# The first pair of a fused attention and feed-forward kernel: f32 and one batch at a time, with zero matmuls in TensorE's gaps

## The chip, the cores and the metric

The kernel runs on one core of a Trainium2 chip. The metric is the time of one execution on the device in microseconds (us), the median over several runs. Engines in the profile: PE is TensorE (matmuls), PEld its weight loads, DVE is VectorE, ACT is ScalarE, POOL is GpSimd, SP issues the DMAs.

## The reference, cut to what matters

There are 16 batches of 64 positions with 512 features. An autocorrelation attention comes first, with a gated residual, then a gated feed-forward part with a second one.

```python
x = x + jnp.tanh(g_xattn[0]) * autocorrelation(layernorm(x), ctx, ctx)   # Q, K, V; 8 heads, C = 2
x = x + jnp.tanh(g_ffn[0]) * ffn(layernorm(x), W_gate, W_up, W_down)

# autocorrelation, for every feature on its own, over L = 64 positions
corr = ifft(fft(q) * conj(fft(k))).real
w, idx = top_k(corr, 8);  w = softmax(w)
out = sum over i of w[i] * v[min(idx[i] + pos, L - 1)]
# ffn: 512 -> 1792 -> 512, weights in f16
h = silu(x @ W_gate.T) * (x @ W_up.T);  out = h @ W_down.T
```

## The kernel before, in words

Two batches of 64 rows fill the 128 partitions: this is a pair, and there are eight pairs, 0 to 7. All data of f32 accuracy goes to TensorE as two f16 halves, high and low. ScalarE makes the high half by a copy, GpSimd (or VectorE, where ON_VECTOR says so) makes the low half by subtracting. A product with a constant matrix, itself split in two, is then three f16 matmuls: high by high, low by high, high by low. The steps of one pair, by the names in the code:

- stats1, rstd1, q_norm: layernorm of x. q_hi, q_lo, k_hi, k_lo: the split of the normed x and of ctx.
- kspec, vspec, qspec (`transform`, L757): spectra of k, v and q, each six matmuls of 64 rows by 512 columns. The two batches of a pair lie in rows 0 to 63 and 64 to 127, so their matmuls use different halves of the array. kcopy, vcopy: ScalarE copies the spectra out of PSUM.
- prod, p_hi, p_lo, lags (L836 to L838): product of the spectra, split, and 24 matmuls of 64 columns that give the correlation.
- max, match, exp, sum, scale: the eight best lags of every row by VectorE (MAX8, MATCH_REPLACE8), their softmax on ScalarE, VectorE and GpSimd.
- wt, w_hi, w_lo for pair 0: transpose of the weights on TensorE. For the others w_rows_hi, w_rows_lo, w_t: split first, then two transposing DMAs.
- wspec, mix_prod, m_hi, m_lo, mix (L897): spectra of the weights, product with those of v, split, and 12 matmuls back to positions. residual: x1 = x + gate * result, with the second layernorm's sums.
- rstd2, xn, then xt, x_hi, x_lo (pair 0, by TensorE) or x_rows_hi, x_rows_lo, x_t (the others, by DMA): the normed x1, transposed and split.
- gate, up (`widen`, L773): 14 tiles of 128 hidden features in four steps by SPANS, each tile of each of the two weight matrices eight matmuls with 128 moving columns (the 128 tokens of the pair). tanh, silu, hid, h_hi, h_lo: the activation and its split. down (L937): 28 matmuls of 512 columns. out, store.

ORDER is one long list written into the file, in which the steps of several pairs are interleaved. Every engine walks the same list, takes the steps that are its own and does them strictly in that order, with semaphores between engines. So a step that waits holds back all later steps on its engine. PSUM has eight banks, assigned by hand (`k_bank` and the like), and a step also waits until its bank is free. SP first issues all loads (x and ctx of pair 0, f32 constants, x and ctx of pair 1, the f16 constants `consts`, then the weights `wg`, `wu`, `wd`), and then, in ORDER's place, the transposing DMAs and stores. The f32 constants `consts32` are loaded in the version before too, though nothing uses them there.

Of the kernel before, what the change touches and what calls it, by code (L numbers as in the profile page):

```python
# [114 lines left out]
mix_prod:0 exp:1 kspec:2 mix_prod:0.1 wspec:0.1 m_hi:0 sum:1 kcopy:2 m_hi:0.1 mix_prod:0.2 scale:1 mix:0
mix_prod:0.3 m_hi:0.2 m_lo:0 m_lo:0.1 m_hi:0.3 w_rows_hi:1 mix:0.1 scales:0 m_lo:0.3 m_lo:0.2 kcopy:2.1 w_t:1
vspec:2 stats1:3 w_rows_lo:1 mix:0.2 vcopy:2 residual:0 vcopy:2.1 rstd1:3 k_hi:3 qspec:2 w_t:1.1 prod:2
rstd2:0 prod:2.1 p_hi:2 xn:0 p_hi:2.1 p_lo:2 q_norm:3 xt:0 p_lo:2.1 x_hi:0 stats1:4 wspec:1 q_hi:3 x_lo:0
rstd1:4 lags:2 mix_prod:1 gate:0 q_lo:3 max:2 m_hi:1 m_lo:1 mix_prod:1.1 up:0 match:2 m_hi:1.1 k_lo:3 tanh:0
k_hi:4 gate:0.1 k_lo:4 silu:0 exp:2 m_lo:1.1 wspec:1.1 sum:2 kspec:3 mix_prod:1.2 scale:2 up:0.1 kcopy:3 hid:0  # L120
kcopy:3.1 mix_prod:1.3 tanh:0.1 vspec:3 m_hi:1.2 silu:0.1 w_rows_hi:2 m_lo:1.2 q_norm:4 gate:0.2 m_hi:1.3
w_t:2 hid:0.1 vcopy:3 m_lo:1.3 vcopy:3.1 mix:1 h_hi:0 mix:1.1 w_rows_lo:2 mix:1.2 tanh:0.2 qspec:3 residual:1
k_hi:5 h_lo:0 w_t:2.1 up:0.2 h_hi:0.1 prod:3 rstd2:1 silu:0.2 p_hi:3 gate:0.3 h_lo:0.1 prod:3.1 up:0.3
tanh:0.3 hid:0.2 p_lo:3 p_hi:3.1 xn:1 wspec:2 p_lo:3.1 down:0 silu:0.3 x_rows_hi:1 hid:0.3 h_hi:0.2 x_t:1
mix_prod:2 h_lo:0.2 m_hi:2 lags:3 h_hi:0.3 down:0.1 q_hi:4 x_rows_lo:1 max:3 h_lo:0.3 mix_prod:2.1 x_t:1.1
down:0.2 match:3 m_lo:2 m_hi:2.1 q_lo:4 down:0.3 wspec:2.1 m_lo:2.1 exp:3 kspec:4 mix_prod:2.2 gate:1 sum:3
m_hi:2.2 kcopy:4 m_lo:2.2 mix_prod:2.3 kcopy:4.1 up:1 tanh:1 scale:3 m_hi:2.3 silu:1 m_lo:2.3 stats1:5
w_rows_hi:3 vspec:4 w_t:3 hid:1 mix:2 k_lo:5 vcopy:4 mix:2.1 out:0 vcopy:4.1 mix:2.2 store:0 w_rows_lo:3
h_hi:1 qspec:4 gate:1.1 prod:4 rstd1:5 w_t:3.1 residual:2 up:1.1 tanh:1.1 rstd2:2 p_hi:4 silu:1.1 prod:4.1
p_lo:4 gate:1.2 hid:1.1 p_hi:4.1 xn:2 h_hi:1.1 p_lo:4.1 wspec:3 tanh:1.2 h_lo:1 x_rows_hi:2 up:1.2 mix_prod:3  # L130
x_t:2 mix_prod:3.1 m_hi:3 h_lo:1.1 silu:1.2 m_hi:3.1 lags:4 m_lo:3 hid:1.2 gate:1.3 max:4 h_hi:1.2 up:1.3
tanh:1.3 h_lo:1.2 stats1:6 down:1 x_rows_lo:2 silu:1.3 match:4 m_lo:3.1 down:1.1 x_t:2.1 hid:1.3 wspec:3.1
h_hi:1.3 kspec:5 exp:4 h_lo:1.3 mix_prod:3.2 down:1.2 mix_prod:3.3 m_hi:3.2 q_norm:5 m_hi:3.3 m_lo:3.2 sum:4
gate:2 q_hi:5 kcopy:5 scale:4 down:1.3 tanh:2 m_lo:3.3 kcopy:5.1 up:2 silu:2 w_rows_hi:4 out:1 w_t:4
w_rows_lo:4 vspec:5 hid:2 rstd1:6 mix:3 h_hi:2 mix:3.1 q_lo:5 k_hi:6 mix:3.2 vcopy:5 gate:2.1 residual:3
w_t:4.1 vcopy:5.1 stats1:7 up:2.1 rstd2:3 tanh:2.1 q_norm:6 h_lo:2 xn:3 qspec:5 rstd1:7 wspec:4 prod:5
gate:2.2 silu:2.1 p_hi:5 prod:5.1 k_hi:7 p_lo:5 hid:2.1 p_hi:5.1 up:2.2 q_norm:7 tanh:2.2 p_lo:5.1 x_rows_hi:3
mix_prod:4 h_hi:2.1 x_t:3 k_lo:6 gate:2.3 silu:2.2 store:1 q_hi:6 hid:2.2 lags:5 x_rows_lo:3 h_hi:2.2 up:2.3
max:5 tanh:2.3 h_lo:2.1 m_hi:4 down:2 silu:2.3 x_t:3.1 mix_prod:4.1 h_lo:2.2 hid:2.3 m_hi:4.1 down:2.1 match:5
q_lo:6 m_lo:4 down:2.2 m_lo:4.1 exp:5 kspec:6 q_hi:7 sum:5 wspec:4.1 h_hi:2.3 kcopy:6 h_lo:2.3 gate:3  # L140
mix_prod:4.2 scale:5 m_hi:4.2 k_lo:7 w_rows_hi:5 down:2.3 kcopy:6.1 up:3 m_lo:4.2 out:2 tanh:3 mix_prod:4.3
store:2 w_rows_lo:5 w_t:5 silu:3 m_hi:4.3 gate:3.1 hid:3 m_lo:4.3 vspec:6 tanh:3.1 mix:4 vcopy:6 w_t:5.1
mix:4.1 vcopy:6.1 mix:4.2 h_hi:3 up:3.1 residual:4 h_lo:3 silu:3.1 gate:3.2 rstd2:4 hid:3.1 xn:4 qspec:6
x_rows_hi:4 wspec:5 prod:6 h_hi:3.1 x_t:4 x_rows_lo:4 up:3.2 tanh:3.2 prod:6.1 p_hi:6 silu:3.2 p_lo:6
mix_prod:5 gate:3.3 hid:3.2 m_hi:5 h_lo:3.1 up:3.3 mix_prod:5.1 x_t:4.1 p_hi:6.1 h_hi:3.2 down:3 p_lo:6.1
tanh:3.3 m_hi:5.1 silu:3.3 hid:3.3 h_lo:3.2 wspec:5.1 lags:6 m_lo:5 mix_prod:5.2 down:3.1 mix_prod:5.3
m_hi:5.2 max:6 h_hi:3.3 m_hi:5.3 h_lo:3.3 down:3.2 match:6 m_lo:5.1 q_lo:7 gate:4 m_lo:5.2 exp:6 down:3.3
sum:6 kspec:7 out:3 scale:6 up:4 kcopy:7 m_lo:5.3 tanh:4 kcopy:7.1 silu:4 gate:4.1 w_rows_hi:6 hid:4 w_t:6
w_rows_lo:6 vspec:7 tanh:4.1 mix:5 vcopy:7 mix:5.1 vcopy:7.1 mix:5.2 h_hi:4 w_t:6.1 up:4.1 residual:5 h_lo:4
silu:4.1 rstd2:5 qspec:7 hid:4.1 gate:4.2 prod:7 h_hi:4.1 xn:5 p_hi:7 wspec:6 p_lo:7 prod:7.1 x_rows_hi:5  # L150
up:4.2 tanh:4.2 x_t:5 mix_prod:6 x_rows_lo:5 p_hi:7.1 mix_prod:6.1 silu:4.2 p_lo:7.1 gate:4.3 hid:4.2
wspec:6.1 h_lo:4.1 h_hi:4.2 x_t:5.1 m_hi:6 up:4.3 store:3 tanh:4.3 m_lo:6 lags:7 silu:4.3 down:4 max:7
h_lo:4.2 mix_prod:6.2 down:4.1 hid:4.3 match:7 h_hi:4.3 m_hi:6.1 gate:5 m_hi:6.2 m_lo:6.1 h_lo:4.3
mix_prod:6.3 down:4.2 tanh:5 m_lo:6.2 m_hi:6.3 exp:7 m_lo:6.3 up:5 sum:7 scale:7 down:4.3 mix:6 out:4
w_rows_hi:7 mix:6.1 mix:6.2 w_t:7 gate:5.1 residual:6 silu:5 up:5.1 rstd2:6 hid:5 w_rows_lo:7 xn:6 h_hi:5
gate:5.2 tanh:5.1 h_lo:5 w_t:7.1 silu:5.1 store:4 hid:5.1 up:5.2 tanh:5.2 x_rows_hi:6 silu:5.2 h_hi:5.1 x_t:6
x_rows_lo:6 gate:5.3 hid:5.2 h_lo:5.1 wspec:7 down:5 mix_prod:7 mix_prod:7.1 m_hi:7 x_t:6.1 tanh:5.3 m_lo:7
up:5.3 m_hi:7.1 silu:5.3 h_hi:5.2 wspec:7.1 m_lo:7.1 down:5.1 mix_prod:7.2 h_lo:5.2 hid:5.3 m_hi:7.2
mix_prod:7.3 m_lo:7.2 gate:6 m_hi:7.3 h_hi:5.3 m_lo:7.3 down:5.2 tanh:6 h_lo:5.3 silu:6 mix:7 mix:7.1 mix:7.2
down:5.3 up:6 out:5 residual:7 gate:6.1 hid:6 rstd2:7 up:6.1 xn:7 tanh:6.1 silu:6.1 x_rows_hi:7 h_hi:6 x_t:7  # L160
gate:6.2 x_rows_lo:7 hid:6.1 h_hi:6.1 h_lo:6 up:6.2 tanh:6.2 h_lo:6.1 silu:6.2 x_t:7.1 gate:6.3 store:5
hid:6.2 up:6.3 h_hi:6.2 tanh:6.3 h_lo:6.2 down:6 silu:6.3 hid:6.3 h_hi:6.3 h_lo:6.3 down:6.1 gate:7 down:6.2
tanh:7 down:6.3 up:7 out:6 silu:7 store:6 gate:7.1 hid:7 h_hi:7 h_lo:7 up:7.1 tanh:7.1 silu:7.1 gate:7.2
hid:7.1 up:7.2 tanh:7.2 h_hi:7.1 silu:7.2 h_lo:7.1 gate:7.3 hid:7.2 up:7.3 h_hi:7.2 tanh:7.3 h_lo:7.2 down:7
# [805 lines left out]
```

## Time and profile before

| | us |
|---|---|
| median of three runs | 234.69 |
| lowest and highest | 233.81, 235.1 |
| the profiled execution | 235.26 |
| its span in the trace | 233.4 |
| PE busy in the span | 208.3 |
| DVE busy in the span | 149.0 |
| POOL busy in the span | 139.9 |

The profile is one execution. Its own time is 1.86 us above its span (start and end outside the traced part) and 0.57 us above the median. A busy PE in this profile is one that has matmuls under way, since matmuls overlap; the rate has to be read from the starts of two neighbouring ones.

### The profile page before, as it was taken

The page shows a single profiled execution, that of the slowest core. Times are in us where ns is not written, and L with a number is a line of the kernel's source. Part 1 is how long each engine was busy: PE and PEld are TensorE (multiplying, and loading weights), DVE is VectorE, ACT ScalarE, POOL GpSimd, SP SyncE. Part 2 cuts the span into 40 slices and gives each one's busy share as a digit, 9 for nine tenths or more (in the row PEclk, how much of TensorE's full clock was granted, in tenths as well). Part 3 has the DMA queues.
Part 4 walks back from the last instruction along what each step waited for, and adds up shares of the span by engine and source line. Part 5 has one row for each costly group of instructions (what it writes and reads, how often), then busy time and mean ns, then how long its engine had stood idle before and what let it go on. Part 6 is the DMA issues. An engine that isn't in the chain of part 4 may idle for free.

```text
span 233.4 us, 6265 instructions
## 1 busy us (share of the span) xinstructions
PE 208.3 (89%) x2552; PEld 144.6 (62%) x2552; DVE 149.0 (64%) x423; ACT 102.6 (44%) x197; POOL 139.9 (60%) x150
## 2 busy tenths in 40 slices
...
PEclk9998556799999999999999999999999999999999
...
GB/s 171 282 447 430 382 90 45 0 4 25 22 49 0 94 25 22 3 45 3 94 0 94 14 34 3 22 25 93 1 1 47 93 0 3 91 2 47 4 0 45
DMA packets 19883, 16.64 MB, mean 71 GB/s; under 512 B 15888, under 2 KB 16272, under 8 KB 19472
## 3 DMA queue, kind: packets, MB, share of 16 engines
...
q14 instruction: 7, 0.06, 0.1%
...
## 4 chain that ended last, share of the span: by engine, by line
PE 86%; DVE 4%; DMA 2%; POOL 2%; ACT 2%; SPq 1%; issue 1%
PE psum L773 44%; PE psum L937 21%; PE psum L757 13%; PE psum L897 5%; DMA consts<-table 2%; POOL prod_lo L473 2%; PE psum L836 1%; DVE probs L653 1%; PE psum L838 1%; PE psum L837 1%; SPq L400 1%; DVE prod L631 1%; ACT prod_hi L539 1%; ACT mixed_hi L577 1%; ACT kv_spec L527 0%
## 5 line engine op out<-in xcount | busy, mean ns | idle before, releaser
L773 PE MATMUL psum<-xt_hi,wg 128*128 128x128 f16 x448 | 53.7, 220 | 0.0
L773 PE MATMUL psum<-xt_lo,wg 128*128 128x128 f16 x448 | 53.6, 219 | 0.0
L773 PE MATMUL psum<-xt_hi,wu 128*128 128x128 f16 x448 | 53.6, 219 | 0.0
L773 PE MATMUL psum<-xt_lo,wu 128*128 128x128 f16 x448 | 53.5, 219 | 0.0
L501 POOL TENSOR_TENSOR hid_lo<-hid,hid_hi 128x512 f16<-128x512 f32 (+1 forms) x32 | 33.5, 1049 | 26.6 <-ACT hid_hi L594 26.6
L773 PEld LDWEIGHTS psum<-xt_hi,wu 128*128 128x128 f16 x448 | 43.6, 98 | 4.5 <-issue 3.8
L773 PEld LDWEIGHTS psum<-xt_hi,wg 128*128 128x128 f16 x448 | 43.7, 98 | 4.0 <-issue 3.4
L773 PEld LDWEIGHTS psum<-xt_lo,wu 128*128 128x128 f16 x448 | 43.8, 98 | 0.7
L773 PEld LDWEIGHTS psum<-xt_lo,wg 128*128 128x128 f16 x448 | 43.9, 98 | 0.6
L937 PE MATMUL psum<-wd,hid_hi 128*128 128x512 f16 x112 | 42.5, 379 | 0.0
L937 PE MATMUL psum<-wd,hid_lo 128*128 128x512 f16 x112 | 42.4, 379 | 0.0
L482 POOL TENSOR_TENSOR mixed_lo<-mixed,mixed_hi 128x512 f16<-128x512 f32 x30 | 35.5, 1189 | 9.5 <-ACT mixed_hi L577 9.3
L594 ACT ACTIVATE hid_hi<-hid 128x512 f16<-128x512 f32 (+1 forms) x32 | 18.3, 572 | 29.7 <-DVE hid L744 29.7
L735 DVE SCALAR_TENSOR_TENSOR act<-act,psum 128x512 f32<-128x512 f32 (+1 forms) x32 | 19.6, 613 | 17.1 <-ACT act L587 17.0
L587 ACT ACTIVATE act<-psum 128x512 f32<-128x512 f32 (+1 forms) x32 | 17.2, 538 | 28.2 <-PE psum L773 28.2
L577 ACT ACTIVATE mixed_hi<-mixed 128x512 f16<-128x512 f32 x32 | 19.9, 626 | 19.3 <-DVE mixed L685 19.3
L685 DVE SCALAR_TENSOR_TENSOR mixed<-psum,kv_spec 128x512 f32<-128x512 f32 x32 | 21.2, 681 | 9.5 <-PE psum L757 9.5
L757 PE MATMUL psum<-k_hi,consts 64*128 64x512 f16 x64 | 14.5, 456 | 11.1 <-DMA consts<-table 9.4
L473 POOL TENSOR_TENSOR prod_lo<-prod,prod_hi 128x512 f16<-128x512 f32 x15 | 18.5, 1239 | 7.7 <-ACT prod_hi L539 7.7
L744 DVE TENSOR_TENSOR hid<-act,psum 128x512 f32<-128x512 f32 (+1 forms) x32 | 19.8, 618 | 4.8 <-PE psum L773 2.6
L937 PEld LDWEIGHTS psum<-wd,hid_hi 128*128 128x128 f16 x112 | 10.9, 98 | 13.0 <-issue 1.7
L748 DVE SCALAR_TENSOR_TENSOR x_sb<-psum,scales,x_sb 128x512 f32<-128x512 f32 x8 | 6.0, 749 | 18.8 <-PE psum L937 18.8
...
## 6 DMA issues: line engine op xcount, KB each, us to landing
...
wg<-w_gate SPq DMA_DIRECT2D x1, 1792.0 KB, 11.0
wu<-w_up SPq DMA_DIRECT2D x1, 1792.0 KB, 14.8
wd<-w_down SPq DMA_DIRECT2D x1, 1792.0 KB, 18.7
...
```

What stands on the lines that cost most here:

```text
L473: nc.gpsimd.tensor_tensor(prod_lo[:, e, n, :], prod[:, e, n, :], prod_hi[:, e, n, :], ALU.subtract).then_inc(split_sems["p_lo", False], 1)
L482: nc.gpsimd.tensor_tensor(mixed_lo[:, e, n, :], mixed[:, e, n, :], mixed_hi[:, e, n, :], ALU.subtract).then_inc(split_sems["m_lo", False], 1)
L501: nc.gpsimd.tensor_tensor(hid_lo[:, e, first:end, :].rearrange("p a t -> p (a t)"), hid32[:, n % 2, 0:(end - first) * P], hid_hi[:, e, fir ...
L577: nc.scalar.activation(mixed_hi[:, e, n, :], mixed[:, e, n, :], ACT.Copy).then_inc(mixed_high, 1)
L587: nc.scalar.activation(act32[:, n % 2, 0:cols], psum[:, gate_bank(p, n), 0:cols], ACT.Tanh, scale=0.5).then_inc(tanh_done, 1)
L594: nc.scalar.activation(hid_hi[:, e, first:end, :].rearrange("p a t -> p (a t)"), hid32[:, n % 2, 0:(end - first) * P], ACT.Copy).then_inc( ...
L685: nc.vector.scalar_tensor_tensor(mixed[:, e, n, :], psum[:, w_bank(p, m, b), :], MIX_UP, kv_spec[:, e, n, :], ALU.mult, ALU.mult).then_inc ...
L735: nc.vector.scalar_tensor_tensor(a, a, 1.0, psum[:, gate_bank(p, n), 0:cols], ALU.add, ALU.mult).then_inc(silu_done, 1)
L744: nc.vector.tensor_tensor(hid32[:, n % 2, 0:cols], act32[:, n % 2, 0:cols], psum[:, up_bank(p, n), 0:cols], ALU.mult).then_inc(hid_done, 1)
L757: last = nc.tensor.matmul(psum[:, banks[b], :], consts[rows(b), forward(name, part)], data[rows(b), :], start=data is high and part == 0, ...
L773: last = nc.tensor.matmul(psum[:, bank, a * P:(a + 1) * P], w[:, k, m * P:(m + 1) * P], xt[:, e, k, :], start=(k == 0 and part == 0), stop ...
L937: last = nc.tensor.matmul(psum[:, down_bank(p), :], hid[:, e, m, :], wd[:, m, :], start=(m == 0 and part == 0), stop=(m == MT - 1 and part ...
```

## The change

Only pair 0 is computed in another way; for the other pairs the order of the steps and a few buffers differ.

- Pair 0 goes through kspec, qspec, vspec, lags, wspec and mix as f32 matmuls on `consts32`, one in place of three f16 ones. The splits k_hi, k_lo, q_hi, q_lo, p_hi, p_lo, w_lo, m_hi and m_lo of pair 0 are gone.
- From lags on, pair 0 is done batch by batch: lags, max, sub, match, exp, sum, scale, wt, w_hi, wspec, mix, residual, rstd2, xn, xt, x_hi, x_lo. The weights of a batch are transposed to 64 partitions, so that both batches use rows 0 to 63 in wspec.
- The feed-forward part of pair 0 is done for the 64 tokens of one batch at a time: the matmuls of `widen` have 64 moving columns and are twice as many. The steps are BATCH_SPANS; every step is 8 or 6 tiles of 64 columns.
- Three times TensorE does matmuls on a tile of zeros (`nothing`, set by VectorE at the start): 12 before all else, 4 after the second half of lags, 9 after kspec of pair 1, each with 512 columns. They write to banks that nobody reads then.
- The subtraction of the largest value (sub) is a step of its own ahead of match, so that exp can start earlier.
- `xn_hi` and `xn_lo` have one buffer in place of two.
- ORDER is a new list, with feed-forward and attention steps of the pairs interleaved in another way, and gate of pair 0 placed ahead of the spectra of pair 2.

```diff
-SPANS = ((0, 4), (4, 8), (8, 12), (12, 14))
-STEPS = len(SPANS)
+STEPS = 4
+SPANS = ((0, 4), (4, 8), (8, 12), (12, 14))
+BATCH_SPANS = ((0, 8), (8, 14), (0, 8), (8, 14))
+DOWN_SPANS = ((0, 4), (4, 8), (8, 11), (11, 14))
...
 ORDER = """
-stats1:0 rstd1:0 k_hi:0 k_lo:0 q_norm:0 stats1:1 q_hi:0 k_hi:1 q_lo:0 rstd1:1 kspec:0 k_lo:1 q_norm:1 qspec:0
-kcopy:0 kspec:1 kcopy:0.1 prod:0 vspec:0 prod:0.1 p_hi:0 p_hi:0.1 p_lo:0 stats1:2 vcopy:0 kcopy:1 lags:0
...
+warm:0 stats1:0 rstd1:0 q_norm:0 kspec:0 qspec:0 kcopy:0 stats1:1 kcopy:0.1 vspec:0 prod:0 rstd1:1 vcopy:0
+prod:0.1 lags:0 k_hi:1 q_norm:1 lags:0.1 warm:0.1 vcopy:0.1 k_lo:1 max:0 gates:0 scales:0 sub:0 kspec:1
+warm:0.2 match:0 exp:0 k_hi:2 max:0.1 kcopy:1 sum:0 q_hi:1 scale:0 kcopy:1.1 q_lo:1 sub:0.1 wt:0 vspec:1
+match:0.1 w_hi:0 exp:0.1 stats1:2 wspec:0 vcopy:1 sum:0.1 wspec:0.1 rstd1:2 vcopy:1.1 mix_prod:0 qspec:1
+scale:0.1 prod:1 wt:0.1 mix:0 mix_prod:0.2 w_hi:0.1 p_hi:1 prod:1.1 mix:0.1 q_norm:2 p_lo:1 p_hi:1.1 wspec:0.2
+residual:0 q_hi:2 p_lo:1.1 wspec:0.3 lags:1 mix_prod:0.1 rstd2:0 mix_prod:0.3 mix:0.2 k_lo:2 xn:0 max:1 xt:0
+q_lo:2 mix:0.3 x_hi:0 k_hi:3 x_lo:0 sub:1 gate:0 k_lo:3 match:1 exp:1 tanh:0 sum:1 kspec:2 up:0 residual:0.1
+kcopy:2 scale:1 kcopy:2.1 w_rows_hi:1 stats1:3 rstd2:0.1 vspec:2 w_t:1 silu:0 gate:0.1 w_rows_lo:1 vcopy:2
+xn:0.1 vcopy:2.1 rstd1:3 qspec:2 k_hi:4 xt:0.1 w_t:1.1 prod:2 tanh:0.1 up:0.1 k_lo:4 prod:2.1 p_hi:2 silu:0.1
...
-ON_VECTOR = (("m_lo", 0, 1), ("m_lo", 0, 3), ("p_lo", 0, 1), ("q_lo", 0, 0), ("scale", 0, 0), ("scale", 0, 1),)
+ON_VECTOR = (("scale", 0, 0), ("scale", 0, 1),)
...
+WARM_UP = ((12, 4), (4, 7), (9, 7))
...
+    nothing = hid_lo[:, 1, 0:4, :].rearrange("p a t -> p (a t)")
...
     def gate_bank(p, s):
-        return 2 * ((p + s) % 2)
+        return (0, 6, 0, 2)[s] if p == 0 else 2 * ((p + s) % 2)
...
+            nc.vector.memset(nothing, 0.0).then_inc(nothing_set, 1)
...
-            def widen(w, bank, e, span):
+            def widen(w, bank, e, span, tok):
+                n = tok.stop - tok.start
                 for a, m in enumerate(range(*span)):
                     for k in range(KT):
                         for part, xt in enumerate((xt_hi, xt_lo)):
-                            last = nc.tensor.matmul(psum[:, bank, a * P:(a + 1) * P], w[:, k, m * P:(m + 1) * P],
-                                                    xt[:, e, k, :], start=(k == 0 and part == 0),
+                            last = nc.tensor.matmul(psum[:, bank, a * n:(a + 1) * n], w[:, k, m * P:(m + 1) * P],
+                                                    xt[:, e, k, tok], start=(k == 0 and part == 0),
                                                     stop=(k == KT - 1 and part == 1))
...
+                if step == "warm":
+                    count, bank = WARM_UP[n]
+                    pe.wait_ge(nothing_set, 1)
+                    if n > 0:
+                        pe.wait_ge(prod_done, 2)
+                    for _ in range(count):
+                        nc.tensor.matmul(psum[:, bank, :], nothing[:, 0:P], nothing, start=True, stop=True)
                 if step == "kspec":
...
-                    if whole("k", p):
+                    if p == 0:
                         pe.wait_ge(whole_first, 16)
-                        pe.wait_ge(ctx_loaded[load_of(p)], 16)
+                        pe.wait_ge(ctx_loaded[0], 16)
                         last = transform32(banks, "even_kv", ctx_sb[:, p, :])
...
+                if step == "lags" and p == 0:
+                    pe.wait_ge(whole_loaded, 16)
+                    pe.wait_ge(prod_done, n + 1)
                     for c in range(CH):
+                        last = nc.tensor.matmul(psum[:, lag_bank(p, n), (2 * c + n) * L:(2 * c + n + 1) * L],
+                                                prod[:, e, n, c * P:(c + 1) * P],
+                                                consts32[:, WHOLE_LAG0:WHOLE_LAG0 + L], start=True, stop=True)
+                    last.then_inc(lags_done, 1)
...
+                if step == "wspec" and p == 0:
+                    b, m = n // 2, n % 2
+                    pe.wait_ge(w_high, nth("w_hi", p, b))
+                    if m == 0:
+                        pe.wait_ge(v_copied, b + 1)
+                    else:
+                        pe.wait_ge(prod_done, b + 1)
+                    nc.tensor.matmul(psum[:, w_bank(p, m, b), :], consts32[0:L, forward32(("even", "odd")[m])],
+                                     w_whole[:, b, :], start=True, stop=True).then_inc(w_spectra, 1)
...
+                if step == "mix" and p == 0:
+                    b, m = n // 2, n % 2
+                    pe.wait_ge(mixed_done, nth("mix_prod", p, 2 * m + b))
+                    last = nc.tensor.matmul(psum[rows(b), mix_bank(p, b), :], mix_matrix32(m), mixed[:, e, 2 * m + b, :],
+                                            start=m == 0, stop=m == 1)
...
                 if step == "gate":
+                    span, tok = ffn_step(p, n)
+                    if p == 0:
+                        if n % 2 == 0:
+                            pe.wait_ge(xt_low, nth("x_lo", p, n // 2))
...
```

## Rows read from the trace of the kernel before

**Rows 1.** The page's summary: busy time and the span in 40 slices.
```profile
PE 208.3 (89%) x2552; PEld 144.6 (62%) x2552; DVE 149.0 (64%) x423; ACT 102.6 (44%) x197; POOL 139.9 (60%) x150
...
PEclk9998556799999999999999999999999999999999
```

**Rows 2.** Stretches: length, busy PE, PEld, DVE, ACT, POOL, granted clock, DMA.
```profile
7.82:45.16 37.34, 23.25 (x165) 9.03 (x166) 31.67 (x99) 19.51 (x39) 20.96 (x24) 0.73 0.64 243
45.16:230.23 185.07, 185.05 (x2392) 135.54 (x2389) 115.11 (x320) 80.36 (x155) 116.54 (x119) 1.00 0.14 30
230.23:233.40 3.17, 0.00 (x0) 0.00 (x0) 0.75 (x1) 0.00 (x0) 0.00 (x0) 0.98 0.22 83
```

**Rows 3.** The two longest of PE's waits: us in total, times, longest.
```profile
PE psum L757 <- DMA consts<-table: 9.4, 1, 9.4
PE psum L836 <- POOL prod_lo L473: 4.8, 3, 4.2
```

**Rows 4.** The chain that ended last: start, length, what.
```profile
71.64 3.68 PE psum L773 x64
75.32 0.75 PE psum L757 x6
76.07 1.42 PE psum L897 x12
```

**Rows 5.** Timeline of PE: start, length, line, form, count.
```profile
13.61 0.63 PE L757 MATMUL psum<-k_lo,consts 64*128 64x512 f16 x2
14.04 0.63 PE L757 MATMUL psum<-k_hi,consts 64*128 64x512 f16 x2
...
18.67 0.39 PE L757 MATMUL psum<-q_hi,consts 64*128 64x512 f16 x2 [1.05 <-POOL q_lo L469]
18.89 0.39 PE L757 MATMUL psum<-q_lo,consts 64*128 64x512 f16 x2
...
65.06 0.19 PE L836 MATMUL psum<-consts,prod_hi 128*128 128x64 f16 x1
...
65.76 0.38 PE L937 MATMUL psum<-wd,hid_hi 128*128 128x512 f16 x1
```

**Rows 6.** Timeline of PE's weight loads: the four f32 transposes of xn.
```profile
41.51 0.42 PEld L905 LDWEIGHTS psum<-ident,xn 128*128 128x128 f32 x4 [2.75 <-DVE xn L712]
```

**Rows 7.** Timeline of DVE: stats1 of pair 1, then pair 0's softmax.
```profile
7.82 0.69 DVE L600 BATCH_NORM_STATS2 raw_stats<-x_sb 128x6 f32<-128x512 f32 x1 [1.70 <-DMA x_sb<-x]
...
15.43 0.63 DVE L641 MAX8 top<-psum 128x8 f32<-128x64 f32 x4
...
17.23 0.18 DVE L656 TENSOR_TENSOR expo<-top 128x32 f32<-128x32 f32 x1
...
20.75 0.17 DVE L661 TENSOR_REDUCE total<-expo 128x4 f32<-128x32 f32 x1
...
21.26 1.29 DVE L617 TENSOR_SCALAR normed<-x_sb,mean_var,rstd 128x512 f32<-128x512 f32 x1
...
23.86 0.72 DVE L669 TENSOR_TENSOR probs<-probs,inv_total 128x256 f32<-128x256 f32 x2
```

**Rows 8.** DVE's groups: count, busy us, mean ns, idle before them.
```profile
L685 DVE SCALAR_TENSOR_TENSOR mixed<-psum,kv_spec 128x512 f32<-128x512 f32 x32 | 21.2, 681 | 9.5 <-PE psum L757 9.5
...
L600 DVE BATCH_NORM_STATS2 raw_stats<-x_sb 128x6 f32<-128x512 f32 x16 | 11.0, 689 | 5.7 <-DMA x_sb<-x 5.4
...
L602 DVE BATCH_NORM_AGGREGATE mean_var<-raw_stats 128x2 f32<-128x6 f32 x16 | 2.9, 182 | 0.5
```

**Rows 9.** The DMA view's issues: KB each, median us from issue to landing.
```profile
wu<-w_up SPq DMA_DIRECT2D x1, 1792.0 KB, 14.8
...
consts<-table SPq DMA_DIRECT2D x1, 128.0 KB, 2.7
...
xt_lo<-xn_lo SPq DMA_TRANSPOSE x7, 2.5
```

**Rows 10.** Timeline of SP: the issue of wu.
```profile
7.38 0.43 SPq L416 DMA_DIRECT2D wu<-w_up  x1
```

More of the change, by code:

```diff
@@ L115 @@
[L115 to L164, printed above, removed]
```

567 lines of the change are left out of this document (305 added, 262 removed).

## The prediction

> **What bounds the kernel now.** I read the summary first [rows 1]: PE is busy for 89% of the span, and the slices show where it isn't, in the first fifth. There the granted clock falls too. The second view splits the span at the first matmul of pair 0's feed-forward part, at 45.16 us [rows 2]. From there to the last matmul, 185.07 us, PE is never idle, at full clock; behind it lie 3.17 us of last addition and store. Ahead of it, from 7.82 to 45.16, PE has 23.25 of 37.34 us under way at a mean granted clock of 0.73, while DVE is busy for 31.67, or 85%. So the kernel is two things in a row: a front that waits on a chain through all engines, and a long stretch that is the sum of TensorE's work. The waits say what the front lacks [rows 3]: 9.4 us for the f16 constants and 4.8 us for POOL's low halves of the products. A change to the first pair pays by the time at which PE becomes continuously busy, and costs by the TensorE work that then still lies ahead.
>
> **Unit prices of TensorE at full clock.** 64 matmuls of `widen` take 3.68 us, 0.0575 each; six of `transform` take 0.75, twelve of mix 1.42 [rows 4]. The 24 matmuls of 64 columns in lags run from 65.06 to 65.76, 0.029 each [rows 5]. 512 columns take 0.22: two matmuls on separate halves of the array start at 18.67, the next two at 18.89. At 13.61 and 14.04 they are 0.43 apart, which is 1.2 GHz, although the page grants full speed there [rows 1, 5]; I go by the starts.
>
> **What the change does to the front.** The wait for `consts` goes: pair 0 needs `consts32` and ctx, issued before it, and the first part of the f32 table lands in 2.7 us [rows 9]. The twelve zero matmuls take 12 x 0.43 = 5.2 us at 1.2 GHz, from about 1 to about 6.3 us. They hold back kspec of pair 0 by a us at most, and in the rows before it took about as much work to reach the fast rate (0.43 apart still at 14.04, 0.22 at 18.67 [rows 5]).
>
> An f32 matmul of 512 columns is not in this trace, except that f32 transposes of 128 columns are: four weight loads in 0.42 us, under 0.11 each, twice the f16 0.0575 [rows 6]. Lower bound: one pass, 0.22. Upper bound: the split kernel computes three of the four products of high and low halves; if the engine forms all four, 4 x 0.22 = 0.86. I take 0.86, nearer to the doubled transposes than one pass is. kspec, qspec and vspec are pairs on separate halves, 0.86 each step if they run side by side as in f16, 1.7 if not. wspec and mix of pair 0 are eight single ones, 6.9 us, where two `transform` and one mix cost 2 x 0.75 + 1.42 = 2.9. The eight f32 lags lie between 8 x 0.029 and, by four weight loads each, 8 x 0.42; I take 2.0. The Trainium skill (FP8 and Floating Point Precision, TensorE Precision Notes) gives true f32 four passes through the array; no row here shows it, and the sum by it would be the same.
>
> These prices don't set the front, because DVE does. Its work from stats1 of pair 1 at 7.82 (x lands then, as before) to x_lo of the first batch, by the new list:
> - softmax of pair 0: two times max, match and sub, 15.43 to 17.41, 1.98 each; two sums at 20.75 to 21.26, 0.51 each; scale 0.72 in all [rows 7]: 5.7
> - prod of pairs 0 and 1 and mix_prod of pair 0, 8 x 0.68 [rows 8]: 5.4; residual of batch 0, taken as one more: 0.7
> - statistics, three times 0.69 + 0.18 [rows 8]: 2.6
> - three normalisations (q_norm 1 and 2, xn) at the 1.29 of [rows 7]: 3.9
> - max of pair 1, 2 x 0.63: 1.3; x_lo on half the columns, 0.35
>
> Together 19.9, so gate of pair 0 starts at 27.7 if DVE never waits. If DVE is busy for only 85% of the time, as before [rows 2], it is 23.5 us: 31.3. I take 29.0, nearer to the lower end, since the waits on POOL's halves are gone for pair 0 and one batch's work fills the other's waits. The removed splits of pair 0 are no term of their own: they are simply not in the list. `wu`, issued at 7.38, lands 14.8 us later, at 22.2, before it is needed [rows 9, 10]. The memset of `nothing` lies in DVE's idle time before x arrives. So the long stretch starts 16.2 us sooner.
>
> **What is moved into the long stretch.** Gate of pair 0 now precedes things that were done by 45.16: k, v and q spectra of pair 2 (3 x 0.75), its lags (0.70), the first half of wspec of pair 1 (0.75), transposes of the second batch (4 x 0.1 at most), 4.1 us. `widen` of pair 0 becomes 448 matmuls of 64 columns: 448 x 0.029 = 13.1 in place of 224 x 0.0575 = 12.9, +0.2. Work ahead: 185.07 + 4.3 = 189.4. The zero matmuls all lie before it (the last 13 take 2.9 us while pair 0's softmax keeps TensorE waiting) and cost nothing there; without that cover they would cost those 2.9.
>
> **A new wait in it.** Pair 1 must be ready sooner. From gate of pair 0 to gate of pair 1 the list gives PE 13.1 (widen), 28 x 0.22 = 6.2 (down), ten transforms (7.5), two lags (1.4), mix (1.4), 0.4: 30.0 us. DVE's list until xn of pair 1: softmax of pairs 1 and 2 without max of pair 1, some 7.9 (twice the halves of [rows 7]); prod, mix_prod, silu, hid and residual, 16 x 0.68 = 10.9; four statistics 3.5; three normalisations 3.9; x_lo 0.35: 26.5 us. Then come two splits, about 1.5 by my allowance, and the transposing DMA, 2.5 [rows 9]: 30.5. So the gap is 0.5 us with a DVE that never waits, and 5.2 with one at 85%. I take 2.0. The same wait holds back tanh and the copies queued behind it on ScalarE, but PE is the only one that counts. Later pairs have in their favour that DVE is busy for only 115.11 of 185.07 [rows 2]. One buffer for `xn_hi` in place of two adds a wait on a transfer of 2.5 us issued a whole pair earlier: nothing.
>
> **Sum.** 29.0 + 189.4 + 2.0 + 3.2 = 223.6 us of span against 233.4, 9.8 less. The profiled execution took 235.26 (1.86 above its span), 0.57 above the median. So 225.5 for a like execution, and 224.9 against the median of 234.69.
>
> **Rivals.**
> - *A: the zero matmuls don't hold the clock.* The granted clock fell before after gaps in PE's work [rows 1]. If TensorE is at 1.2 GHz from wt of pair 0 on (at 7.82 + 7.0 = 14.8 by the list above), its work until gate of pair 0, two spectra 1.5, wspec and mix 6.9, lags 0.7, transposes 1.2, is 10.3 at full speed and 20.6 at half: gate at 35.4, 6.4 later, 231.3. For it: half of the first pair's new work is single f32 matmuls with waits between. Against: 10.3 of 14.2 us is a share of 0.7, and 2.9 us of zeros fill the time just before.
> - *B: the gain is given back behind the front.* Both DVE bounds at their upper ends, 31.3 and 5.2: 5.5 later, 230.4. For it: DVE stood at 85% in the front and POOL has as much to do. Against: after 45.16 DVE had 62%, and PE never waited.
> - *C, slower than before: 64 columns cost as much as 128.* At L773, if a matmul is bounded by its weight load or its issue and not its columns, 448 x 0.0575 = 25.8 in place of 13.1: +12.7, 237.6. It decides from 0.051 us per matmul upward, where 9.8 us are eaten. For it: lags show 24 in a row, not 448, and those may have been queued up. Against: 0.029 with a new weight load each [rows 5]. A section of the Trainium skill bears on it (TensorE: Matmul & The Clock Gate, "Wait — 56ns, not 53.3ns?"): with decode by the sequencer's program a matmul takes about 62 ns to issue, else the floor is about 25. By 62 it would be 27.8 us, 239.6; the 0.0575 and the 0.029 of the rows speak for the floor.
>
> **How the numbers follow.** The forecast as costed 0.73, B 0.10, A 0.10, C 0.07. The time is 224.9. Its own range goes from both lower ends, 27.7 and 0.5 (222.1), to near B. Below 222.1 lies what I priced high, three plus three normalisations at 1.29 that may take half: 219.5. Above, B's 230.4 and A's 231.3: 231.5. That leaves C and a share of A out. What can be told from no change is about 0.5%, 1.2 us: 233.5 to 235.9. All cases but C are faster than that: 0.92; same 0.02; slower 0.06.
>
> **What the profile after would show.** First `widen` matmul at 27.7 to 31.3 us, its 64-column matmuls 0.029 apart (C: 0.0575); f32 matmuls of 512 columns 0.86 apart; granted clock at full from 7 us on (A: half between 15 and 30); DVE over 85% busy from 7.8 to 29; PE's idle time ahead of gate of pair 1 of 0.5 to 5 us and none later; the last matmul 3.2 us before the end. The prediction is wrong if PE waits repeatedly in the new list after pair 1, of which the trace of before says nothing.

## The result and the profile after

| | before | after |
|---|---|---|
| median, us | 234.89 (4 runs) | 226.44 (4 runs, 226.15 to 227.02) |
| ratio | | 0.9646 (0.9601 to 0.9691) |
| profiled execution, us | 235.26 | 226.31 |
| its span, us | 233.4 | 224.5 |
| first matmul of pair 0's gate, us | 45.16 | 28.91 |

Forecast were 224.9, in 219.5 to 231.5. One timed run of a later kernel (f32 alone, 236.31 us) was in a slower state and is left out of its median and ratio below.

The summary and the slices of the page, against [rows 1]:

```profile
PE 215.6 (96%) x2787; PEld 149.6 (67%) x2787; DVE 149.8 (67%) x424; ACT 98.4 (44%) x191; POOL 134.2 (60%) x148
...
PE   7899699799999999999999999999999999999994
...
PEclk9999979999999999999999999999999999999999
```

PE is busy for 60% of a slice or more from the first to the last but one, and the granted clock dips in one slice only. The same split into stretches as in [rows 2] follows, with the stretch around the dip taken apart (length, busy PE, PEld, DVE, ACT, POOL, granted clock, DMA). Its border is 28.98, where the page's chain of work puts the first gate step; the first matmul of it starts at 28.91.

```profile
7.59:28.98 21.39, 18.47 (x105) 7.84 (x102) 21.07 (x67) 9.77 (x22) 10.08 (x13) 0.97 0.97 387
...
25.00:27.00 2.00, 0.18 (x2) 0.04 (x1) 2.00 (x3) 0.00 (x0) 1.62 (x2) 1.00 1.01 382
27.00:29.00 2.00, 2.00 (x8) 0.56 (x9) 2.00 (x11) 0.90 (x2) 0.56 (x1) 0.68 1.05 384
29.00:31.00 2.00, 2.00 (x40) 2.00 (x41) 2.00 (x16) 0.77 (x2) 0.59 (x1) 0.50 0.70 259
...
28.98:221.30 192.32, 190.96 (x2665) 139.15 (x2664) 126.29 (x354) 86.19 (x166) 123.06 (x129) 0.99 0.16 34
221.30:224.50 3.20, 0.00 (x0) 0.00 (x0) 0.75 (x1) 0.00 (x0) 0.00 (x0) 1.00 0.22 82
```

The front is 16.2 us shorter, the long stretch 7.3 us longer than the 185.07 of [rows 2], the tail the same: 8.9 us of span. In the front DVE is busy for 21.07 of 21.39 us. All waits of PE of over half a us, against [rows 3]:

```profile
PE psum L949 <- DVE xn L769: 1.8, 1, 1.8
PE psum L838 <- DVE hid_lo L641: 1.2, 1, 1.2
PE psum L877 <- DVE prod L675: 0.9, 1, 0.9
PE psum L889 <- POOL prod_lo L512: 0.7, 1, 0.7
PE psum L808 <- DVE xt_lo L780: 0.6, 1, 0.6
```

The 9.4 us for the f16 constants are gone, and the 4.8 for POOL are down to 0.7. The timeline of PE, against [rows 5]: the 12 zero matmuls, two f32 spectra, the f32 lags, the transposes of xn, and `widen` on 64 columns at its start and behind the dip:

```profile
1.17 4.06 PE L838 MATMUL psum<-hid_lo 128*128 128x512 f16 x12 [1.17 <-DVE hid_lo L641]
5.51 1.13 PE L816 MATMUL psum<-ctx_sb,consts 64*128 64x512 f32 x4 [0.28 <-DMA ctx_sb<-ctx]
6.44 1.05 PE L816 MATMUL psum<-normed,consts 64*128 64x512 f32 x4
7.30 1.05 PE L816 MATMUL psum<-ctx_sb,consts 64*128 64x512 f32 x4
9.24 1.97 PE L877 MATMUL psum<-consts,prod 128*128 128x64 f32 x16 [0.88 <-DVE prod L675]
...
26.96 0.46 PE L949 MATMUL psum<-ident,xn 64*128 64x64 f32 x4 [1.82 <-DVE xn L769]
...
28.91 0.23 PE L825 MATMUL psum<-xt_hi,wg 128*128 128x64 f16 x1
28.96 0.24 PE L825 MATMUL psum<-xt_lo,wg 128*128 128x64 f16 x1
...
32.67 0.19 PE L825 MATMUL psum<-xt_lo,wu 128*128 128x64 f16 x1
32.70 0.19 PE L825 MATMUL psum<-xt_hi,wu 128*128 128x64 f16 x1
```

An f32 matmul appears as two records. From 6.44 to 7.30 a whole spectrum, two matmuls on separate halves of the array, takes 0.86 us. The lags take 2.0 us for eight. The 64-column matmuls are 0.03 apart at 32.67 and 0.05 at 28.91, in the dip: the 64 of the first up step start from 32.63 to 34.48, which is 0.029 each.

What VectorE's 21.07 us hold is seen only beside GpSimd. First VectorE's three normalisations in the front, then GpSimd's list at the same time:

```profile
9.61 1.42 DVE L662 TENSOR_SCALAR normed<-x_sb,mean_var,rstd 128x512 f32<-128x512 f32 x1
...
20.47 1.38 DVE L662 TENSOR_SCALAR normed<-x_sb,mean_var,rstd 128x512 f32<-128x512 f32 x1
...
24.54 2.37 DVE L769 TENSOR_SCALAR xn<-x_sb,mean_var,rstd 64x512 f32<-64x512 f32 x1
```

```profile
20.42 2.44 POOL L512 TENSOR_TENSOR prod_lo<-prod,prod_hi 128x512 f16<-128x512 f32 x2 [2.17 <-ACT prod_hi L587]
...
24.36 1.15 POOL L504 TENSOR_TENSOR k_lo<-ctx_sb,k_hi 128x512 f16<-128x512 f32 x1
25.48 1.15 POOL L508 TENSOR_TENSOR q_lo<-normed,q_hi 128x512 f16<-128x512 f32 x1
```

xn starts at 24.54, 0.18 us behind the start of GpSimd's k_lo, and ends at 26.91, when q_lo has ended too, at 26.63. The same instruction takes 0.54 us elsewhere (below). So some 3.5 of the 21.07 us (1.42, 1.38 and 2.37, less 0.54 each) are VectorE being held, not working. One subtraction of the softmax adds 0.6: it takes 0.82 us at 14.66, beside GpSimd's q_lo of 14.28 to 15.44, and 0.18 at 11.94, with GpSimd idle.

### The profile page after: what moved, and what is told of

Its sections match the earlier page's. It is cut to its first block, busy times and chain, and to the rows that moved or that the text cites. A ratio compares the mean times of both kernels' runs of the same rounds, so it can differ in the third digit from the quotient of the medians.

```text
span 224.5 us, 6750 instructions
## 1 busy us (share of the span) xinstructions
PE 215.6 (96%) x2787; PEld 149.6 (67%) x2787; DVE 149.8 (67%) x424; ACT 98.4 (44%) x191; POOL 134.2 (60%) x148
## 4 chain that ended last, share of the span: by engine, by line
PE 89%; DVE 4%; DMA 2%; POOL 1%; issue 1%; SPq 1%; ACT 0%; DVEq 0%
PE psum L825 46%; PE psum L990 22%; PE psum L808 11%; PE psum L941 4%; DMA x_sb<-x 2%; PE psum L838 1%; DVE xn L769 1%; POOL prod_lo L512 1%; DVE prod L675 1%; PE psum L877 1%; PE psum L908 1%; PE psum L889 1%; PE psum L926 1%; DVE raw_stats L644 1%; PE psum L891 1%
## 5 line engine op out<-in xcount | busy, mean ns | idle before, releaser
L825 PE MATMUL psum<-xt_hi,wg 128*128 128x128 f16 (+1 forms) x504 | 54.9, 215 | 0.0
L825 PE MATMUL psum<-xt_lo,wg 128*128 128x128 f16 (+1 forms) x504 | 54.8, 215 | 0.0
L825 PE MATMUL psum<-xt_hi,wu 128*128 128x128 f16 (+1 forms) x504 | 54.0, 213 | 0.0
L825 PE MATMUL psum<-xt_lo,wu 128*128 128x128 f16 (+1 forms) x504 | 53.9, 213 | 0.0
L550 POOL TENSOR_TENSOR hid_lo<-hid,hid_hi 128x512 f16<-128x512 f32 (+2 forms) x32 | 33.5, 1051 | 26.7 <-ACT hid_hi L635 26.6
L787 DVE SCALAR_TENSOR_TENSOR act<-act,psum 128x512 f32<-128x512 f32 (+2 forms) x32 | 19.6, 612 | 23.9 <-ACT act L628 23.9
L628 ACT ACTIVATE act<-psum 128x512 f32<-128x512 f32 (+2 forms) x32 | 17.2, 538 | 32.7 <-PE psum L825 32.6
L635 ACT ACTIVATE hid_hi<-hid 128x512 f16<-128x512 f32 (+2 forms) x32 | 18.3, 572 | 22.3 <-DVE hid L795 22.3
L795 DVE TENSOR_TENSOR hid<-act,psum 128x512 f32<-128x512 f32 (+2 forms) x32 | 19.7, 619 | 9.7 <-PE psum L825 8.1
L990 PEld LDWEIGHTS psum<-wd,hid_lo 128*128 128x128 f16 x112 | 11.0, 98 | 11.0
```

The lines of the kernel that those rows point to most:

```text
L550: nc.gpsimd.tensor_tensor(hid_lo[:, e, first:end, tok], hid32[:, n % 2, 0:ffn_cols(p, n)].rearrange("p (a t) -> p a t", a=end - first), hi ...
L628: nc.scalar.activation(act32[:, n % 2, 0:cols], psum[:, gate_bank(p, n), 0:cols], ACT.Tanh, scale=0.5).then_inc(tanh_done, 1)
L635: nc.scalar.activation(hid_hi[:, e, first:end, tok], hid32[:, n % 2, 0:ffn_cols(p, n)].rearrange("p (a t) -> p a t", a=end - first), ACT.C ...
L787: nc.vector.scalar_tensor_tensor(a, a, 1.0, psum[:, gate_bank(p, n), 0:cols], ALU.add, ALU.mult).then_inc(silu_done, 1)
L795: nc.vector.tensor_tensor(hid32[:, n % 2, 0:cols], act32[:, n % 2, 0:cols], psum[:, up_bank(p, n), 0:cols], ALU.mult).then_inc(hid_done, 1)
L825: last = nc.tensor.matmul(psum[:, bank, a * n:(a + 1) * n], w[:, k, m * P:(m + 1) * P], xt[:, e, k, tok], start=(k == 0 and part == 0), st ...
```

## The experiments

The ratio is to the kernel before, timed on the same chip. Span and gate are those of the one profiled execution; "gate" is the start of the first `widen` matmul of pair 0. It varies by itself: the kernels of "GpSimd order" and "next chain" have the same list up to gate, and it starts at 26.51 and 27.08. Medians of different kernels come from different chips in part, on which the kernel before took 234.89 to 235.21, so a few tenths of a us between them say nothing.

| run | median, us | ratio (95%) | span | gate |
|---|---|---|---|---|
| the change | 226.44 | 0.9646 (0.9601 to 0.9691) | 224.5 | 28.91 |
| no zeros | 227.0 | 0.9654 (0.9608 to 0.9699) | 225.3 | 29.53 |
| first 12 left out | 227.14 | 0.9665 (0.9606 to 0.9725) | 225.2 | 29.43 |
| later 13 left out | 228.13 | 0.9705 (0.9651 to 0.9758) | 226.2 | 30.94 |
| GpSimd order | 224.96 | 0.9582 (0.9539 to 0.9625) | 222.8 | 26.51 |
| gap filled | 226.99 | 0.9652 (0.9618 to 0.9687) | 224.6 | 28.77 |
| both | 225.3 | 0.9584 (0.9549 to 0.9618) | 223.6 | 27.27 |
| f32 alone | 232.78 | 0.9895 (0.9809 to 0.9981) | 232.6 | 44.18 |
| zeros alone | 233.7 | 0.9927 (0.9893 to 0.996) | 230.4 | 42.26 |
| f32 and zeros | 230.69 | 0.9814 (0.9756 to 0.9873) | 229.4 | 41.31 |
| next chain | 224.77 | 0.9561 (0.9521 to 0.9601) | 223.1 | 27.08 |
| VectorE more | 226.59 | 0.9643 (0.9592 to 0.9694) | 224.6 | 28.21 |
| TensorE more | 228.27 | 0.9727 (0.9673 to 0.9781) | 226.5 | 30.39 |

### Taking the zero matmuls out

```diff
-WARM_UP = ((12, 4), (4, 7), (9, 7))
+WARM_UP = ((0, 4), (0, 7), (0, 7))     # no zeros
+WARM_UP = ((0, 4), (4, 7), (9, 7))     # first 12 left out
+WARM_UP = ((12, 4), (0, 7), (0, 7))    # later 13 left out
```

> The changed kernel without any of its 25 zero matmuls (its own time 226.4 us, first feed-forward matmul at 28.98 us). Theory 'the zeros hold the clock': TensorE starts pair 0 at 1.2 GHz, the three f32 spectra take 1.7 us each instead of 0.86, and with idle places at 11 to 15 us it does not get to or keep 2.4 GHz before the feed-forward part; the 10.3 us of work between wt of pair 0 and gate double, gate of pair 0 starts 6 us later, at about 35, and the kernel takes about 232. Rival 'VectorE sets the front, the zeros are ornament': the f32 work is dense enough by itself, gate of pair 0 at 29 to 30, 226 to 227.5.

> Only the first 12 zero matmuls left out, the 4 and 9 stay. Theory 'the zeros hold the clock': kspec, qspec and vspec of pair 0 take 1.7 us each, prod starts at about 8.9 in place of 8.4 and max of the first batch about 1.7 us later; from then on at full speed: gate of pair 0 at about 31, 228.4 us. Rival 'the late ones are what counts': at most 0.5 us, 226.4 to 226.9, since VectorE has other work in that time.

> The first 12 zero matmuls stay, the 4 and 9 behind lags and kspec of pair 1 are left out. Theory 'the zeros hold the clock': TensorE is idle for 3 us between 11 and 14.7 us, the clock falls, and wspec, mix and the spectra of pair 1 run at 1.2 GHz: gate of pair 0 4 to 6 us later, 230.5 to 232.5. Rival 'the f32 work keeps it busy enough': the clock stays, gate of pair 0 at 29, 226.4 or a little less.

Without any zeros the kernel is 0.6 us slower by the medians and 0.2 by the ratios, with intervals that overlap; the rival had it right. PE's timeline of that run:

```profile
5.61 2.08 PE L816 MATMUL psum<-ctx_sb,consts 64*128 64x512 f32 x4 [5.61 <-DMA ctx_sb<-ctx]
7.45 1.94 PE L816 MATMUL psum<-normed,consts 64*128 64x512 f32 x4
9.15 1.71 PE L816 MATMUL psum<-ctx_sb,consts 64*128 64x512 f32 x4
10.79 2.00 PE L877 MATMUL psum<-consts,prod 128*128 128x64 f32 x16
...
29.53 0.20 PE L825 MATMUL psum<-xt_hi,wg 128*128 128x64 f16 x1
```

The f32 spectra do take the 1.2 GHz price: by the starts 1.84, 1.70 and 1.64 us, though the granted clock reads 1.00 there. From the lags on the work goes at the fast rate (1.97 us for the same lags in the change, 2.00 here), and it stays there to the gate and beyond, over idle times of 0.6, 1.6 and 1.8 us.

Leaving out only the first 12 cost 0.7 us by the medians, less than the theory's 2.0 and a little more than the rival's 0.5. Leaving out only the later 13 is the dearest of the three, 1.7 us by the medians, where the theory said 4 to 6 and the rival nothing. The clock falls twice. The first fall stands behind the longest wait, which in the run without any zeros comes later and is shorter, as the slower spectra have used up the time. The row of that wait in the run without the later 13, then in the run without any:

```profile
PE psum L898 <- DVE probs L722: 2.8, 1, 2.8
```

```profile
PE psum L898 <- issue: 1.6, 1, 1.6
```

Behind the 2.8 us the granted clock is 0.50 from 16 to 18 us, and the transposes of xn start at 28.65, 1.7 us later than in the change. So here a TensorE that was warmed and then left idle fared worse than one that was never warmed.

What decides the second fall, behind the wait for xn, stays open. That wait is 1.8 us in the change and in all three of these runs. The clock fell behind it in the change (all four timed runs have a mean granted clock of 0.992) and in the run without the later 13. It did not fall in the profiles of the two others, nor in that of "TensorE more" below, which has all 25 zeros and the same wait. And one timed run without the first 12 has 0.992 too. So the first 12 zeros don't decide it.

### The wait for xn and the dip

```diff
 # GpSimd order: three words moved in ORDER
-... q_lo:1 sub:0.1 ... p_hi:1.1 wspec:0.2 residual:0 q_hi:2 p_lo:1.1 ... rstd2:0 ... k_lo:2 ... q_lo:2
+... q_lo:1 k_lo:2 sub:0.1 ... p_hi:1.1 q_hi:2 wspec:0.2 residual:0 p_lo:1.1 q_lo:2 ... rstd2:0 ...
 # gap filled: zero matmuls in the wait (eight; four in the run of both)
-WARM_UP = ((12, 4), (4, 7), (9, 7))
+WARM_UP = ((12, 4), (4, 7), (9, 7), (8, 5))
-... mix:0.2 k_lo:2 ...
+... mix:0.2 warm:0.3 k_lo:2 ...
```

> The changed kernel with three steps moved in the list: k_lo of pair 2 behind q_lo of pair 1, q_hi and q_lo of pair 2 ahead of rstd2 of pair 0. In the changed kernel xn of pair 0's first batch took 2.37 us, the time in which GpSimd did k_lo and q_lo of pair 2 (24.36 to 26.63 us). Theory 'GpSimd holds VectorE back': with GpSimd idle xn takes its 0.55 us, rstd2 comes 0.5 us later, gate of pair 0 starts 1.4 us earlier, and as TensorE then waits for under 0.5 us the clock does not fall, which gives another 1 to 1.8 us: 223.3 to 225.0. Rival 'xn on 64 rows is slow by itself': xn again over 2 us, and gate of pair 0 where it was or 0.5 us later, 226.4 to 227.

> The changed kernel with eight more zero matmuls behind mix:0.2, in the 1.8 us in which TensorE waits for xn. Theory 'that wait costs the clock': the granted clock stays at 1.0 from 25 to 31 us, the second f32 mix takes 0.86 in place of 1.6 us and the first gate step 1.9 in place of 2.96: 1.8 us less, 224.6. Rival 'VectorE and the loads are the bound there anyway': the 64-column matmuls are faster but the next steps wait, 226.0 to 226.6.

> Both edits, with four zero matmuls. If both theories hold, gate of pair 0 starts at about 27 us at full clock: 223.0 to 223.6. If only the zeros help, 224.6; if only the GpSimd order helps, as that run.

GpSimd held VectorE back. With its order changed, xn starts at the same time and takes a quarter of it. VectorE's timeline of the run with the GpSimd order, then GpSimd's:

```profile
9.28 0.54 DVE L662 TENSOR_SCALAR normed<-x_sb,mean_var,rstd 128x512 f32<-128x512 f32 x1
...
24.52 0.54 DVE L769 TENSOR_SCALAR xn<-x_sb,mean_var,rstd 64x512 f32<-64x512 f32 x1 [0.25 <-POOL rstd L485]
```

```profile
9.46 1.37 POOL L504 TENSOR_TENSOR k_lo<-ctx_sb,k_hi 128x512 f16<-128x512 f32 x1 [0.33 <-ACT k_hi L565]
```

Gate moves to 26.51, 2.4 us earlier: 1.8 by xn and the rest by the clock, which doesn't dip. The kernel gains 1.5 us by the medians, just inside what was expected. At 9.28 it is the other way round: the normalisation starts first and takes its 0.54 us, and GpSimd's k_lo, started within it, takes 1.37 us instead of the 1.16 of the change. The Trainium skill (SBUF — State Buffer, "SBUF: two separate sides") tells of one port pair shared by VectorE, in the modes that need a second pair, and GpSimd: whichever starts first locks it for its whole instruction. 0.54 against 2.37 us agrees, and so does k_lo's 1.37; in which mode VectorE's instruction ran, no run shows.

One of the five timed runs had a mean granted clock of 0.992, as the change has, and took 226.76 us; the four others took 224.42 to 225.1. There is no trace of it, so what a dip costs in this order stays open.

Filling the gap also removed the dip, and gained nothing: 226.99, as its rival said, if a little above the rival's 226.0 to 226.6. The next transform, kspec of pair 2, starts at the same time with the dip and without it. PE's timeline of the change, then of the run with the gap filled:

```profile
31.88 0.39 PE L808 MATMUL psum<-k_hi,consts 64*128 64x512 f16 x2
```

```profile
31.94 0.39 PE L808 MATMUL psum<-k_hi,consts 64*128 64x512 f16 x2 [1.13 <-DVE probs L708]
```

The waits of PE in the run with the GpSimd order:

```profile
PE psum L808 <- DMA w_lo<-w_lo_rows: 1.4, 1, 1.4
...
PE psum L808 <- DVE probs L708: 1.1, 1, 1.1
```

In the change kspec of pair 2 comes up behind a slow gate step, when match of pair 1 has freed its bank; with a fast step TensorE is there 1.1 us too early. At wspec of pair 1 it meets weights that are still on their way: 1.0 us with the gap filled, 1.4 with the GpSimd order. The dip cost nothing in the change, because the time would have been waited. The run with both brought no more than the GpSimd order, and its theory had 223.0 to 223.6.

### The next chain

```diff
 # on top of the GpSimd order, in ORDER
-... gate:0 ... kspec:2 up:0 ... vspec:2 w_t:1 silu:0 gate:0.1 w_rows_lo:1 ...
+... gate:0 ... up:0 kspec:2 ... w_rows_hi:1 w_rows_lo:1 ... gate:0.1 vspec:2 ...
```

> The GpSimd order of the earlier run (its gate of pair 0 started at 26.5 us, and TensorE then waited 1.1 us for the match of pair 1, 0.6 for its first mix_prod and 1.4 for its transposing DMA, span 222.8) with three more steps moved: w_rows_lo of pair 1 right behind w_rows_hi, ahead of rstd2 of the second batch; up:0 ahead of kspec of pair 2; gate:0.1 ahead of vspec of pair 2. Theory 'pair 1's weights are the next thing that is late': the DMA lands about 1 us earlier, the wait for match is filled by up:0, and the span is 221 to 221.8, 223.2 to 224.0 us. Rival 'every move only shifts the wait to the next step, because VectorE is behind all of them': span 222.5 to 223.5, 224.5 to 225.5.

The rival held: 224.77, not to be told from 224.96. The waits for match and for the DMA are gone. In their place TensorE waits 1.3 us for the copies of v's spectra, and again 0.7 us for POOL's products and 0.4 for x_lo of pair 0's second batch, as in the change:

```profile
PE psum L808 <- ACT kv_spec L581: 1.3, 1, 1.3
```

### The parts of the change on the kernel before

```diff
 # f32 alone; the splits of pair 0 and mix:0.2 are taken out of ORDER
-WHOLE = {"k": (), "q": (), "p": (), "w": (), "m": ()}
+WHOLE = {"k": (0,), "q": (0,), "p": (0,), "w": (0,), "m": (0,)}
 # zeros alone: 24, 16 and 6; with f32: 12, 16 and 6
+... warm:0 stats1:0 ... qspec:1 warm:0.1 ... wt:0 warm:0.2 ...
```

> The kernel before with only the f32 part: pair 0 goes through kspec, qspec, vspec, lags, wspec and mix on the f32 constants, its splits are taken out of the list, the order is otherwise the old one, no zero matmuls, both batches together. Theory 'the f32 part removes the 9.4 us wait and POOL's splits from the chain': the first matmul at about 5.3 us, but at 1.2 GHz for long stretches; gate of pair 0 at about 40 in place of 45.2 us, 229 to 231. Rival 'four passes at 1.2 GHz eat what the wait gave': 234 to 236.

> The kernel before with only zero matmuls: 24 at the start, 16 behind qspec of pair 1, 6 behind wt of pair 0. Theory 'the clock is a cost of its own': granted clock at 1.0 until at least 30 us, TensorE's steps of the front halve, gate of pair 0 at 41 to 43, 231 to 233. Rival 'VectorE and POOL set the front': under 1 us, 234 to 235.

> The kernel before with the f32 part and zero matmuls (12, 16 and 6), old order, both batches together. Theory 'f32 and zeros are the change, the batch by batch order adds little': 226.5 to 228.5. Rival 'the batch by batch order with the early gate brings half of the 8.5 us': 229.5 or more, gate of pair 0 at 36 us or later.

f32 alone gained 1.0% by its ratio, some 2.5 us, where the theory said 4 to 6 and the rival nothing. The f16 constants are no longer waited for, but other waits stand in the gap; PE's longest in that run:

```profile
PE psum L834 <- POOL prod_lo L471: 5.7, 2, 5.0
PE psum L763 <- DMA ctx_sb<-ctx: 5.5, 1, 5.5
```

Pair 0 is ahead, and the list then waits for the split products of pair 1. The granted clock was 0.77 from 7.8 to 44.18 us, little better than the 0.73 of [rows 2]. Zeros alone gained 0.7%, between theory and rival. The clock did hold to 30 us as the theory said (granted 1.00 from 7.8 to 30.0, then 0.58 to the gate), so a clock at full through most of the front is worth little by itself. f32 and zeros together gained 1.9%, and the change 3.5%. What is left is the other half, 4.2 us by the medians: the batch by batch form with the new list and the early gate, as that run's rival said. These were not taken apart, and neither of them was run alone.

### Which engine sets the front

```diff
 # VectorE more
+    scratch = sb("scratch", [P, 2, 6])
...
                     layer_stats(e, p, slice(0, P), raw1, stats1, p + 1)
+                    if p == 2:
+                        for i in range(2):
+                            nc.vector.bn_stats(scratch[:, i, :], x_sb[:, p, :])
 # TensorE more: six zero matmuls ahead of wspec:0
+WARM_UP = ((12, 4), (4, 7), (9, 7), (6, 7))
+... warm:0.3 wspec:0 ...
```

> The changed kernel with 1.4 us more work for VectorE at stats1 of pair 2: two more bn_stats of the same rows into a tile that nothing reads. Theory 'VectorE sets the front' (it was busy for 21.07 of the 21.39 us from 7.59 to 28.98): gate of pair 0 at 30.3 and the kernel 1.4 us longer, 227.8. Rival 'the front is a chain through all engines with slack on VectorE': gate at 29.0 to 29.5, 226.4 to 227.

> The changed kernel with 1.3 us more work for TensorE in the front: six more zero matmuls right ahead of wspec of pair 0. TensorE was busy for all of 15 to 20 us. Theory 'VectorE alone sets the front': at most 0.5 us later, 226.4 to 226.9. Rival 'between wt and prod of pair 1 TensorE is as tight as VectorE': gate of pair 0 at 30.0 or later, 227.5 or more.

In the first of these runs the reading of 98% busy fell. With 1.25 us more work for VectorE the time is the same and gate is even earlier. Its timeline:

```profile
9.18 0.54 DVE L666 TENSOR_SCALAR normed<-x_sb,mean_var,rstd 128x512 f32<-128x512 f32 x1
...
16.37 1.25 DVE L659 BATCH_NORM_STATS2 scratch<-x_sb 128x6 f32<-128x512 f32 x2
...
20.75 0.54 DVE L666 TENSOR_SCALAR normed<-x_sb,mean_var,rstd 128x512 f32<-128x512 f32 x1
```

Two normalisations took 0.54 us where they took 1.42 and 1.38 in the change, as they now started ahead of GpSimd's splits and not behind their start. That gives back 1.7 us, more than the 1.25 added. But the first of them, 0.9 us, lies ahead of the added work and can't come from it, and neither can the 0.4 us by which x of pair 1 landed sooner (7.16 against 7.59). The clock doesn't dip in this run either. So it says neither that VectorE has slack nor that it has none; it says that its busy time is no fixed sum.

With 1.3 us more for TensorE gate comes 1.5 us later and the time rises by 1.8. VectorE's timeline shows three waits that the change didn't have in this size, and statistics between them:

```profile
12.35 0.15 DVE L747 TENSOR_SCALAR scales<-gates_tanh 128x1 f32<-128x1 f32 x1 [1.13 <-ACT gates_tanh L601]
...
17.12 0.68 DVE L644 BATCH_NORM_STATS2 raw_stats<-x_sb 128x6 f32<-128x512 f32 x1
...
19.21 0.69 DVE L739 SCALAR_TENSOR_TENSOR mixed<-psum,kv_spec 128x512 f32<-128x512 f32 x1 [0.70 <-PE psum L908]
...
20.73 0.69 DVE L675 TENSOR_TENSOR prod<-psum,kv_spec 128x512 f32<-128x512 f32 x1 [0.49 <-PE psum L808]
```

The last two, 1.2 us, are TensorE's added work passed on: between wt and prod of pair 1 TensorE is as tight as VectorE, and the rival held. The first is not from the edit: ScalarE waited for the DMA of the gates. It has its share in the 1.8 us, since the statistics of pair 2, ahead of what the added work can touch, start 0.9 us later than in the change (17.12 against 16.21), and the first prod of pair 1 2.1 us later (20.73 against 18.67). So just over half of VectorE's delay is the edit's. The clock doesn't dip in this profile, which gives part of it back at gate.

## Why the prediction was right

- **Two parts, front and sum of TensorE's work: right.** Gate was forecast at 29.0 and came at 28.91; the tail at 3.2 and came at 3.2. That gate was hit to 0.1 us is in part luck, by the next point.
- **DVE's list as the front: right in size, only half right as a cause.** The list added to 19.9 us; DVE was busy for 21.07, and idle for 0.3 where 1.3 were allowed. The two errors cancel. Three normalisations at 1.29 were priced as work; they were 0.54 of work and the rest VectorE being held, and xn took 2.37. The lower bound of 27.7 was no bound: the run with the GpSimd order had gate at 26.51. And TensorE stands beside VectorE in part of the front, which the forecast left out.
- **The prices: right.** 0.86 for an f32 spectrum of two matmuls side by side, and 2.0 for the f32 lags were measured as taken. kspec, allowed to be up to a us late by the first zeros, was not held back by them: they took 4.06 us instead of 5.2, it then still waited 0.28 for ctx, and it starts at 5.51, against 5.61 without zeros.
- **Rival C: refuted.** The 64-column matmuls start 0.029 apart in runs of 64, against 0.029 taken and 0.051 where it would have decided. The 62 ns of that section of the Trainium skill (TensorE: Matmul & The Clock Gate, "Wait — 56ns, not 53.3ns?") don't bind here; the 0.029 us lie above its floor of about 25 ns, which no run here reaches.
- **Rival A: refuted.** The granted clock was 1.00 until 27 us and gate came at 28.91, not at 35.4. With the later 13 zeros left out the clock did fall behind wt's wait, from 15 to 19 us, and the loss was 1.7 us by the medians, not 6.4.
- **Rival B: didn't come.** VectorE was at 98% in the front and not at 85%, and the waits behind it were 1.3 us and not 5.2.
- **The long stretch: forecast as 189.4 + 2.0 = 191.4 us, measured 192.3.** It held 1.4 us of idle time (192.32 less 190.96) instead of 2.0. The first gate step, mostly at half clock, took 2.96 us in the page's chain of work where the next one took 1.97: 1.0 more. And that 1.97 is 0.0308 per matmul with the hand-over to the next step, instead of 0.029, which over 448 matmuls is 0.8. Together 192.6, so 0.3 too much; that rest is not explained.
- **The new wait, 2.0 us ahead of gate of pair 1: right in size and stretch, wrong in cause.** It was priced as TensorE waiting for xn of pair 1, and no such wait came. The 1.3 us that TensorE waited stand ahead of gate of pair 1, 0.6 at 40.07 for a bank that x_lo of pair 0's second batch frees and 0.7 at 41.58 for POOL's products of pair 2. In the faster variants it waited for match of pair 1 and the DMA of its weights instead.
- **The zero matmuls "cost nothing": right, and they bring little.** With none at all the time rose by 0.2 to 0.6 us. The clock fell once in the change, for the end of mix and the first gate step, at no net cost.
- **Two slips in the sums.** 448 x 0.029 is 13.0 and not 13.1, and six normalisations at half of 1.29 are 3.9 us, so the lower end by that reasoning would be 218.2 and not 219.5. Neither bears on the outcome.
- The time was 1.5 us above the forecast: 0.9 in the long stretch, the rest in how span, profiled execution and median stand to each other (the median is 1.9 us above the span here, and was taken as 1.3).
